# Attention chain: the row maxima are split into high and low part before their transpose, and one DMA carries both rows

## The reference, cut to what matters

```python
attn = jnp.einsum('bhdi,bhdj->bhij', q * scale, k)      # 8 heads, 1024 x 1024 scores each
attn = jax.nn.softmax(attn, axis=-1)                    # over the 1024 keys
y = jnp.einsum('bhij,bhdj->bhdi', attn, v)
```

## Time and profile before

| | us |
|---|---|
| median of 3 runs | 491.04 (490.61 to 492.54) |
| the profiled execution, its own time | 494.82 |
| its span, first to last instruction | 493.1 |
| PE busy in the span | 466.7 (95%) |
| DVE busy | 361.7 (73%) |
| ACT busy | 270.3 (55%) |
| POOL busy | 209.7 (43%) |

### The profile page before, as it was taken

One profiled execution on the slowest core, in us unless ns is written; L12 is line 12 of the kernel. 1 busy time (PEld: TensorE's weight loads), 2 busy tenths in 40 slices (PEclk: granted clock), 3 DMA queues, 4 the chain that ended last, 5 costly groups with the idle time before them and its releaser, 6 DMA issues.

```text
span 493.1 us, 7075 instructions
## 1 busy us (share of the span) xinstructions
PE 466.7 (95%) x2252; PEld 239.9 (49%) x2252; DVE 361.7 (73%) x684; ACT 270.3 (55%) x518; POOL 209.7 (43%) x195
## 2 busy tenths in 40 slices
PE   8899999999899889999999979989999999999996
PEld 6554444443337656544444423547544444433463
DVE  7799888885653679987777717659998677848673
ACT  3228777776602425876766646033777676866032
POOL 8200031108110003899788950000788788990100
PEclk9959999999897999999999989999999999999999
DMA  5231432103200054587963551015547875353002
GB/s 151 55 60 23 142 57 47 23 5 64 56 10 1 0 122 110 102 193 160 183 155 72 94 93 23 1 48 137 116 104 155 175 148 104 61 101 60 2 2 85
DMA packets 20369, 40.70 MB, mean 83 GB/s; under 512 B 7426, under 2 KB 8586, under 8 KB 20204
## 3 DMA queue, kind: packets, MB, share of 16 engines
q1 hardware_dynamic: 15036, 24.23, 21.0%
q0 software_dynamic: 5152, 16.00, 17.5%
q10 hardware_dynamic: 144, 0.02, 0.0%
HBM read 4.76 MB, written 1.05 MB: 12 GB/s over the span
## 4 chain that ended last, share of the span: by engine, by line
PE 68%; DVE 8%; SPq 8%; DMA 5%; ACT 4%; POOL 4%; issue 3%; ACTq 0%; DVEq 0%; POOLq 0%
PE S L955 16%; PE PV L993 14%; PE S L982 14%; PE S L1107 4%; SPq L326 4%; SPq L319 4%; DVE max L716 3%; POOL SUMS L505 3%; DMA SUMS<-SUMS 3%; PE M L1006 3%; PE PV L907 2%; DMA k_stack<-kL 2%; ACT E L569 2%; PE PV L933 2%; DVE SUMS L747 2%
## 5 line engine op out<-in xcount | busy, mean ns | idle before, releaser
L716 DVE TENSOR_REDUCE max<-S 128x1 f32<-128x512 f32 x384 | 238.9, 674 | 10.9 <-PE S L955 10.2
L569 ACT ACTIVATE E<-S 128x512 f32<-128x512 f32 x384 | 211.0, 605 | 57.0 <-PE S L982 49.6
L505 POOL TENSOR_TENSOR SUMS<-E 128x512 f32<-128x512 f32 x120 | 159.0, 1441 | 121.1 <-ACT E L569 117.6
L955 PE MATMUL S<-k_stack,q_stack 126*128 126x512 f32 x384 | 177.5, 478 | 6.9 <-DMA k_stack<-kL 4.5
L982 PE MATMUL S<-q_stack,k_stack 128*128 128x512 f32 x384 | 155.8, 418 | 5.4 <-ACT E L569 4.6
L955 PEld LDWEIGHTS S<-k_stack,q_stack 126*128 126x128 f32 x384 | 73.3, 193 | 77.5 <-DVE max L716 47.8
L993 PE MATMUL PV<-E,V 128*32 128x512 f32 x768 | 91.6, 598 | 0.0
L982 PEld LDWEIGHTS S<-q_stack,k_stack 128*128 128x128 f32 x384 | 73.2, 193 | 34.8 <-ACT E L569 19.6
L729 DVE TENSOR_TENSOR mHL<-S,mHL 4x128 fp32r<-4x128 f32 x48 | 13.3, 278 | 48.2 <-ACT mHL L558 48.2
L993 PEld LDWEIGHTS PV<-E,V 128*32 128x32 f32 x768 | 20.6, 109 | 46.6 <-issue 26.5
L558 ACT ACTIVATE mHL<-S 4x128 fp32r<-4x128 f32 x48 | 12.7, 264 | 50.2 <-PE S L973 50.2
(11 more groups left out here) (176 smaller groups left out, 339.5 us busy)
## 6 DMA issues: line engine op xcount, KB each, us to landing
SUMS<-SUMS POOLq DMA_DIRECT2D x30, 512.0 KB, 6.1
k_stack<-kH SPq DMA_DIRECT2D x28, 128.0 KB, 3.4
q_stack<-qH SPq DMA_DIRECT2D x40, 64.0 KB, 2.0
rec_sb<-den_sb SPq DMA_DIRECT2D x9, 256.0 KB
q_stack<-qH SPq DMA_DIRECT2D x16, 128.0 KB, 2.4
k_stack<-kL SPq DMA_DIRECT2D x14, 128.0 KB, 4.2
q_stack<-mHL SPq DMA_DIRECT2D x96, 2.0 KB
k_stack<-kH SPq DMA_DIRECT2D x22, 64.0 KB, 2.3
```

The costliest lines, as they stand in the source:

```text
L505: pool.tensor_tensor(SUMS[:, slot, :], E[:, E_PLAN[s][0], :], E[:, E_PLAN[s + 1][0], :], ALU.add).then_inc(sum_ready, 1)
L569: act.activation(E[:, slot, :], B[:, ring_of_scores(s) % B_RING, :], ACT.Exp, scale=1.0 if l == 0 else float(HEAD_DIM[l]) ** -0.5).then_in ...
L716: dve.tensor_reduce(max8[:, m % 2, 2 * t + half:2 * t + half + 1], A[:, n % A_RING, :], AX.X, ALU.max, negate=True).then_inc(a_used, 1)
L955: pe.matmul(A[:, n % A_RING, :], q_stack[0:SHIFT_ROW, slot, q0:q0 + P], k_stack[0:SHIFT_ROW, slot, k0:k0 + HALF], start=True, stop=True).t ...
```

## The change

The split into high and low part moves from behind the transpose to ahead of it. After a unit's eighth maximum, DVE now does three small reductions, each 128 partitions by 8 elements in and 4 out: the maximum of each pair of halves (`most`), the same negated and rounded to fp32r (`high` = -most, rounded), and minus the pairwise sum of both (`low` = -(most + high)). The third waits on the semaphore until the second is done. PE transposes both parts at once, 128 x 8 to 8 x 128. ACT copies all eight rows in one instruction (`shift_out`), which also frees the bank of ring B. `low_rows` goes away, and with it DVE's wait for ACT's copy. SP sends both rows with one DMA a unit (4 KB) in place of two. The steps at which this happens stay where they were.

```diff
-        negmax = sb("negmax", [P, 2, 4])
-        mHL = sb("mHL", [4, 2, 2, P], F32R)
+        mHL = sb("mHL", [8, 2, P], F32R)
+        maxHL = sb("maxHL", [P, 2, 3, 4], F32R)
...
-                for r in range(2):
-                    sp.wait_ge(rows_low if r else rows_high, m + 1)
-                    row = SHIFT_ROW + r
-                    sp.dma_start(q_stack[row:row + 1, slot_of(h), HALF * f:HALF * (f + 1)].bitcast(F32)
-                                 .rearrange("o (t c) -> o t c", t=4),
-                                 mHL[:, m % 2, r, :].bitcast(F32)).then_inc(shift_dma[m % 2], 16)
+                sp.wait_ge(rows_out, m + 1)
+                sp.dma_start(q_stack[SHIFT_ROW:P, slot_of(h), HALF * f:HALF * (f + 1)].bitcast(F32)
+                             .rearrange("r (t c) -> r t c", t=4),
+                             mHL[:, m % 2, :].bitcast(F32)).then_inc(shift_dma[m % 2], 16)
...
-            def high_rows(l, j):
+            def shift_out(l, j):
                 m = UNITS_L * l + j
                 act.wait_ge(rows_done, m + 1)
                 if m >= 2:
-                    act.wait_ge(shift_dma[m % 2], 32 * (m // 2))
-                act.activation(mHL[:, m % 2, 0, :], B[0:4, ring_of_rows(j) % B_RING, 0:P], ACT.Copy).then_inc(rows_high, 1)
+                    act.wait_ge(shift_dma[m % 2], 16 * (m // 2))
+                act.activation(mHL[:, m % 2, :], B[0:8, ring_of_rows(j) % B_RING, 0:P], ACT.Copy).then_inc(rows_out, 1)
...
-                dve.tensor_reduce(max8[:, m % 2, 2 * t + half:2 * t + half + 1], A[:, n % A_RING, :], AX.X, ALU.max,
-                                  negate=True).then_inc(a_used, 1)
+                dve.tensor_reduce(max8[:, m % 2, 2 * t + half:2 * t + half + 1], A[:, n % A_RING, :], AX.X,
+                                  ALU.max).then_inc(a_used, 1)
                 if r == TILES - 1:
                     dve.wait_ge(a_used, n + 1)
                     if m >= 2:
                         dve.wait_ge(rows_done, m - 1)
-                    dve.tensor_reduce(negmax[:, m % 2, :], max8[:, m % 2, :].rearrange("p (t r) -> p t r", r=2), AX.X,
-                                      ALU.min).then_inc(negmax_ready, 1)
-
-            def low_rows(l, j):
-
-                m = UNITS_L * l + j
-                dve.wait_ge(rows_high, m + 1)
-                dve.tensor_tensor(mHL[:, m % 2, 1, :], B[0:4, ring_of_rows(j) % B_RING, 0:P],
-                                  mHL[:, m % 2, 0, :].bitcast(F32), ALU.subtract).then_inc(rows_low, 1)
+                    most, high, low = (maxHL[:, m % 2, part, :] for part in range(3))
+                    pairs = max8[:, m % 2, :].rearrange("p (t r) -> p t r", r=2)
+                    dve.tensor_reduce(most.bitcast(F32), pairs, AX.X, ALU.max).then_inc(max_split, 1)
+                    dve.tensor_reduce(high, pairs, AX.X, ALU.max, negate=True).then_inc(max_split, 1)
+                    dve.wait_ge(max_split, 3 * m + 2)
+                    dve.tensor_reduce(low.bitcast(F32), maxHL[:, m % 2, 0:2, :].bitcast(F32).rearrange("p a t -> p t a"),
+                                      AX.X, ALU.add, negate=True).then_inc(max_split, 1)
...
                 for s in range(-LEAD, STEPS):
-                    if s in ROWS_AT:
-                        low_rows(l, ROWS_AT[s])
...
                 if kind == "rows":
-                    pe.wait_ge(rows_low, UNITS_L * l + at + 1)
+                    pe.wait_ge(rows_out, UNITS_L * l + at + 1)
...
             def transpose_max(l, j):
                 m = UNITS_L * l + j
-                pe.wait_ge(negmax_ready, m + 1)
+                pe.wait_ge(max_split, 3 * (m + 1))
                 ring_free(l, ring_of_rows(j))
-                pe.transpose(B[0:4, ring_of_rows(j) % B_RING, 0:P], negmax[:, m % 2, :], ident[:, :]).then_inc(rows_done, 1)
+                pe.transpose(B[0:8, ring_of_rows(j) % B_RING, 0:P], maxHL[:, m % 2, 1:3, :].rearrange("p a t -> p (a t)").bitcast(F32),
+                             ident[:, :]).then_inc(rows_done, 1)
...
-                    pe.wait_ge(shift_dma[m % 2], 32 * (m // 2 + 1))
+                    pe.wait_ge(shift_dma[m % 2], 16 * (m // 2 + 1))
```

More of the change, by code:

```diff
@@ L194, in attention_chain @@
         a_done, a_used = sem("a_done"), sem("a_used")
-        negmax_ready, rows_done = sem("negmax_ready"), sem("rows_done")
-        rows_high, rows_low = sem("rows_high"), sem("rows_low")
+        rows_done = sem("rows_done")
+        max_split, rows_out = sem("max_split"), sem("rows_out")
         shift_dma = [sem(f"shift_dma{i}") for i in range(2)]
@@ L611, in _ @@
                     project_out(l, n)
-                high_rows(l, 0)
+                shift_out(l, 0)
                 for n in range(6, 8 if l else 6):
@@ L616, in _ @@
                     if s in ROWS_AT:
-                        high_rows(l, ROWS_AT[s])
+                        shift_out(l, ROWS_AT[s])
                     probabilities(l, s)
@@ L713, in maxima @@
                 if r == 0 and m >= 2:
-                    dve.wait_ge(negmax_ready, m - 1)
+                    dve.wait_ge(max_split, 3 * (m - 1))
                 t, half = maxima_tile(i)
-                dve.tensor_reduce(max8[:, m % 2, 2 * t + half:2 * t + half + 1], A[:, n % A_RING, :], AX.X, ALU.max,
-                                  negate=True).then_inc(a_used, 1)
+                dve.tensor_reduce(max8[:, m % 2, 2 * t + half:2 * t + half + 1], A[:, n % A_RING, :], AX.X,
+                                  ALU.max).then_inc(a_used, 1)
                 if r == TILES - 1:
```

## The result

The changed kernel takes 489.22 us (median; 487.42 to 491.27), the kernel before, timed beside it, 491.82. The ratio is 0.994, 95% interval 0.992 to 0.996: 2.6 us faster by the two medians and 3.0 by the ratio, which is that of the means (the kernel before has a tail of runs near 495.6); the forecast was 6.6 (484.4). The sign was right and 489.22 lies in the range, but less than half of the forecast gain is there. The profiled execution took 490.7, its span is 489.0.

A forecast was written before the change was run, and what follows sets the result against it. PE and DVE together were taken to bound the stretch with values. Gains of 3.0, 1.5 and 2.1 us in layers 0 to 2 make 6.6: 494.82 to 488.2, less 3.78 for the median, 484.4 us; range 478.5 to 490.9.

The forecast's parts named there:

- `low_rows` gone, layer 0: Layer 0, stretch with values: DVE no longer waits for ACT's copy, 0.27 us in each of nine intervals, 2.4 us.
- Three small reductions for one: DVE after each unit's maxima: 0.28 us more a unit, free where values run, paid ahead of the first values.
- The starts of layers 1 and 2: Start of each layer: DVE starts 0.27 us earlier, less 0.08 for the unit behind, gain 0.2 each.
- In layer 1 one of the others ends in a wait for the `k_stack` load, which starts when PE has passed a step and so can't shrink: Layer 1, steps 61 to 69: that interval gains nothing; the layer's stretch with values gains 1.3 us.
- One DMA for two: SP's queue: shift DMA lands some 1.28 us earlier at layer 0's start, part of net 0.6; elsewhere no gain.
- Behind step 85 POOL is next: Layers 1 and 2: POOL's 6.22 us a unit limits; no gain counted in layer 1, 0.3 us in layer 2.
- POOL runs without a wait for ACT behind step 85: Sign expected in the changed trace, layers 1 and 2: POOL no longer waits for ACT there; no size given.
- POOL and the DMAs take back layers 1 and 2: Rival: layers 1 and 2 gain nothing, only layer 0's 3.0 us remains, 488.0 us; chance 0.19.
- The slower one: Rival: PE stops at each unit's first score for the shift DMA; 495.6 us at 6.6 us landing; chance 0.10.
- The 3.78: The median shown, 491.04 us, lay 3.78 below the profiled execution's 494.82; the forecast took the same distance.

The follow-up runs named there:

- the later spread: Changed kernel and kernel before, each with the second reciprocal spread sent behind unit 14's rows instead of unit 13's: 484.36 and 494.57 us.
- the second profile: The changed kernel, unaltered, timed and profiled once more beside the kernel before: 489.28 us, ratio 0.994.
- the cut spread: Reciprocal spread cut to 128 of its 512 columns: 486.72 us in the changed kernel, 494.88 us in the kernel before.

## Why the prediction came out as it did

- *`low_rows` gone, layer 0.* Right. Values every 6.20 us (forecast 6.19), the middle 2.37 shorter (2.4), the start 0.6 (0.6). That the start fits is partly luck: it is 21.8 to 23.6 us in the traces of the kernel before and its variants, and 21.0 to 21.8 in those of the changed kernel with one shift DMA and no extra reductions. And the reading of why was half right: moving the instruction out of its wait brought 0.3, so by difference the rest is its own time on DVE.
- *Three small reductions for one.* Right in size (0.35) and in cover: nothing under the values. The starts of layers 1 and 2 lost 0.2 each where the forecast gained 0.2. The run with three more prices it: 0.19 a reduction, paid by four units of a layer. I had netted them against a wait of `low_rows`, but the interval that it stands in didn't shrink (5.38 to 5.43 in layer 1). The Trainium skill, "VectorE: DVE Perf Modes", section "The DRAIN you can't avoid", which the prediction set against the trace, also says there that a next operation that isn't held starts earlier; so a pair 0.08 us apart (83.51, 83.59) is no contradiction to it.
- *"In layer 1 one of the others ends in a wait for the `k_stack` load, which starts when PE has passed a step and so can't shrink."* Wrong for the whole change: the load was held by SP's queue. The interval fell from 7.35 to 6.20, and this is most of why layer 1's middle gained 2.6 and not 1.3. For the split alone it was right: with two DMAs the interval stays (7.47 without the split, 7.55 with it, both with the later spread).
- *One DMA for two.* The mechanism was named, the term mis-sized: "past the layer starts SP has idle time ahead of each" was read from the shift DMA alone, without asking which loads stand behind it. 0.6 forecast, 6.8 measured without the meeting (3.3 with it: 492.55 to 489.22).
- *The split.* 6.6 less the DMA's 0.6 is 6.0 forecast, 3.4 measured with the later spread in both kernels, and nothing that can be told without it (1.000).
- *"Behind step 85 POOL is next."* This is the step that took the gain away: the ends of the layers were put at nothing but the shift of what stands before them, and the end of layer 2 gave back 5.4. Two facts were on the rows: 12.73 us for the sums in layer 1 and POOL's 3.07 behind it. I read them as POOL being late there and let layer 2 go free. The transfer was slow because the spread had left 0.07 us ahead of it, and layer 2 was free by 0.08 us: there the sums went first (429.33, the spread at 429.41), in layer 1 the spread did (275.43, the sums at 275.50). A change that moves both issues, one on SP and one on POOL, decides that order anew. In the changed kernel the spread led by 1.35 and 0.43 us, and PE waited in both layers, in both profiles. All sixteen such places agree, in layers 1 and 2 of the eight traces whose second spread is one full DMA behind unit 13. Where the spread led (ten places, by 0.07 to 1.35 us) the sums took 10.7 to 12.8 us and PE waited 1.9 to 2.9; where the sums led (six, by 0.05 to 0.37) they took 6.0 to 9.7 and PE didn't wait. No run set the order by itself.
- *POOL runs without a wait for ACT behind step 85.* Those waits, taken over the same stretch, halve (4.6 to 2.4 and 2.5 us), but POOL's time from unit 1's DMA to unit 13's in layer 2 stays at 82 us (81.6 and 82.0), since waits for DMAs take their place; with the later spread it is 79.4.
- *The rivals.* "POOL and the DMAs take back layers 1 and 2" gave 488.0, nearest to 489.2. Its place was right, its mechanism half: the DMAs did it, not POOL's additions, and what came back was lost at two spots and not spread over the layers. The slower one, a shift DMA that lands too late, didn't happen: in the changed kernel's trace PE has no wait for `q_stack<-mHL` that the view lists.
- *The number.* Up to unit 15's transpose of each layer the edit brings 8.0 us by the profiles, so 6.6 was too low for what it does there (the middles 7.1 where 5.6 was forecast, the starts 0.2 where it was 1.0) and too high for what the kernel kept. Errors of opposite sign stand behind it, and it is luck that 489.22 lies in the range. The 3.78 that the forecast took off for the median is near the 3.9 of the meeting in layer 1 of the profiled execution; that they are the same is not shown, as no execution near the median was profiled.
- The Trainium skill, "DMA: Bandwidth & Descriptors", section "Queues, rings and completion order", says that a DMA engine takes turns, packet by packet, between the queues that have work for it. "Why a DMA increments its semaphore by 16 and not by 1" makes the spread run on four engines, by its four source partitions. The sums would then be delayed on those four alone. The slices of the changed kernel shown above agree: 0.2 to 0.3 of the engines (4 of 16 is 0.25) work on alone. No trace shows which engines these were, and no run put the two on different ones.

## What to carry to other kernels

When a change lets the engines run ahead, look for pairs of large transfers on different queues whose issues lie close together, and price what happens if their order flips: here up to 5 us hung on the order of two issues. A DMA removed from a queue is worth what stands behind it in that queue, so list the next loads and how early each is issued ahead of its use. Before keeping or dropping a small gain, move the colliding transfer by one unit: the change was worth 3 us before that, and 7 to 8 with it.

## What the runs showed that was not expected

- The spread of four rows to 32 partitions each takes 7.0 us for 256 KB with no sums beside it and 9.5 where it stands in the chain of the kernel before with the later spread, though 512 KB of sums take 5.9 at the median; four DMAs for it are slower.
- A wait of PE of 2.5 us was followed by up to 2.8 us more at a lower granted clock (1.2 in the second profile, 17.78 for 16.63 from the denominators to the reciprocal). Behind the wait of 1.88 in layer 1 of that profile the granted clock stayed at 1.00.
- Of 48.2 us of DVE waiting, 38.7 could be taken away for 0.3 us in the middle of layer 0 and nothing in the median.
- Less work was not less time: POOL's shorter additions made the changed kernel 3 us slower, and the cut spread the kernel before 3 us.
